# Spreading the depthwise convolution of the next image over five chunks and moving its group norm, tables, offsets and pixels later

## What is computed

```python
# block 0: group norm, 1x1 to 128 channels, a 3x3 depthwise convolution whose
# nine weights per channel come from the pooled image, mish, 1x1 back to 64
xh = conv1x1(gn(x), w_in, b_in)
hcx = relu(mean(xh) @ kg_w1.T + kg_b1)
kernels = (hcx @ kg_w2.T + kg_b2).reshape(b, c, 3, 3)
y = depthwise(xh, kernels)
x = x + conv1x1(y * tanh(softplus(y)), w_out, b_out)
# block 1: group norm again, then a deformable 3x3 convolution
v = gn(x)
offset, mask = conv3x3(v, w_off) + b_off, sigmoid(conv3x3(v, w_mask) + b_mask)
val = bilinear(v, own position + tap + offset) * mask      # nine taps
z = conv1x1(concat(sum_taps(w_def, val), offset, mask), w_1x1) + b_1x1
x = x + silu(batchnorm(z))
```

## Time and profile before

| | |
|---|---|
| median of 3 runs | 5547.52 us (5545.2 to 5550.46) |
| profiled execution | 5541.43 us |
| its span from first to last instruction | 5539.6 us |
| mean granted TensorE clock | 0.815 of full speed |
| busy: PE, DVE, ACT, POOL | 81%, 81%, 47%, 73% |

### The profile page before, as it was taken

How to read it: one execution, slowest core, us unless ns; L and a number is a source line. 1 busy time by engine, 2 the same in 40 slices (tenths; PEclk the granted TensorE clock), 3 DMA queues, 4 the chain that set the end, 5 groups by cost and what they waited for, 6 DMA issues and landing times.

```text
span 5539.6 us, 46074 instructions
## 1 busy us (share of the span) xinstructions
PE 4466.2 (81%) x14774; PEld 1996.3 (36%) x14774; DVE 4498.5 (81%) x5310; ACT 2595.6 (47%) x3580; POOL 4041.9 (73%) x4243
## 2 busy tenths in 40 slices
PE   8688787888878888788887878887778887888874
PEld 3233343433434333333333433333333343333331
...
GB/s 106 103 118 135 103 133 122 120 131 105 141 111 131 123 109 143 104 131 123 116 136 105 133 123 120 133 103 139 115 132 123 110 144 105 131 115 114 122 107 101
DMA packets 280991, 667.35 MB, mean 120 GB/s; under 512 B 76191, under 2 KB 118058, under 8 KB 278506
## 3 DMA queue, kind: packets, MB, share of 16 engines
...
## 4 chain that ended last, share of the span: by engine, by line
PE 36%; DVE 25%; POOL 22%; issue 12%; ACT 3%; DMA 2%; DVEq 0%; POOLq 0%; SPq 0%; ACTq 0%
POOL gat L504 22%; PE yo_ps L774 12%; PE tap_ps L774 7%; DVE gat L1371 5%; PE z_ps L696 5%; DVE pairs L1350 5%; DVE conv_ps L1241 4%; DVE hat_s L1398 4%; PE tap_ps L690 2%; DMA gat<-patch_table,ixu 2%; PE conv_ps L588 2%; PE conv_ps L568 2%; DVE uc L1248 1%; PE xh_ps L756 1%; DVE conv_ps L1238 1%
## 5 line engine op out<-in xcount | busy, mean ns | idle before, releaser
L504 POOL DMA_INDIRECT gat<-patch_table,ixu x4236 | 4033.6, 952 | 1483.6 <-issue 1261.8
L1371 DVE TENSOR_TENSOR gat<-gat,wgt_ps 128x1024 f32<-128x1024 f32 x1059 | 1283.9, 1215 | 445.9 <-DMA gat<-patch_table,ixu 438.7
L1350 DVE TENSOR_REDUCE pairs<-gat 128x256 f32<-128x1024 f32 x1024 | 1239.4, 1210 | 0.0
L774 PE MATMUL yo_ps<-hat_s,hat_image 128*128 128x512 f32 x1860 | 1007.0, 695 | 7.0 <-issue 7.0
L774 PE MATMUL tap_ps<-hat_s,hat_image 128*128 128x512 f32 x1860 | 895.1, 631 | 0.0
L690 PE MATMUL tap_ps<-ident,pairs 128*128 128x128 f32 x2048 | 393.3, 324 | 572.6 <-DVE pairs L1350 572.4
L1039 ACT ACTIVATE val<-tap_ps 128x512 f32<-128x512 f32 x512 | 303.3, 592 | 1087.9 <-PE tap_ps L690 1087.7
L774 PEld LDWEIGHTS yo_ps<-hat_s,hat_image 128*128 128x128 f32 x1860 | 417.5, 232 | 603.5 <-issue 594.2
L1241 DVE SCALAR_TENSOR_TENSOR conv_ps<-xh,kb,conv_ps 128x1024 f32<-128x1024 f32 x480 | 617.5, 1286 | 12.7
L690 PEld LDWEIGHTS tap_ps<-ident,pairs 128*128 128x128 f32 x2048 | 271.1, 163 | 886.1 <-DVE pairs L1350 716.9
L774 PEld LDWEIGHTS tap_ps<-hat_s,hat_image 128*128 128x128 f32 x1860 | 360.5, 202 | 427.6 <-issue 417.8
...
## 6 DMA issues: line engine op xcount, KB each, us to landing
gat<-patch_table,ixu POOLq DMA_INDIRECT x4236, 2.7
...
hat_image<-patch_table SPq DMA_DIRECT2D x144, 128.0 KB
out<-n_z SPq DMA_DIRECT2D x128, 128.0 KB, 2.4
...
```

The lines of the kernel that those rows point to most:

```text
L504: pool.indirect_dma_start(gat[:, k, t * 2 * REC:(t + 1) * 2 * REC], None, table_rows, bass.IndirectOffsetOnAxis(ixu[:, i, k, t:t + 1], 0)) ...
L774: m = pe.matmul(hat_sums[t % 2][:, :], hat_image[:, q // NCH % 2, i, t, :], hat_s[:, i, :], start=(i == 0), stop=(i == HI - 1))
L1350: dve.tensor_reduce(total, gat[:, k, :].rearrange("p (t x c h) -> p t c x h", t=TILES, x=2, h=2), mybir.AxisListType.XY, ALU.add).then_inc ...
L1371: dve.tensor_tensor(patch, patch, wk.rearrange("p (n h) -> p n h", h=2).unsqueeze(2).to_broadcast([128, TILES * 2, C, 2]), ALU.mult).then_ ...
```

## The change

The plans are replaced. The convolution's twelve rows, until now three in each of chunks 0 to 3, are spread over chunks 0 to 4 (3, 3, 2, 2, 2); products, residuals and mish steps follow them; the statistics of the residual become a step of their own (`statistics`), later than the residual; `group_mean` moves from after tap 3 of chunk 4 to its end, `group_var` and `normalise` from chunk 4 to the first two taps of chunk 5; the tables, offsets and pixels stand two to three taps later than before, and `points 0` and `points 1` one tap later. Chunk 7 is as it was.

```diff
+PLAN_CONV = (
+    ((1, "convolve 0 0"), (2, "convolve 0 1"), (4, "convolve 0 2"), (5, "exp 0"), (6, "ln 0"), (7, "tanh 0"), (8, "project 0")),
+    ((1, "residual 0"), (2, "convolve 1 0"), (4, "convolve 1 1"), (7, "convolve 1 2"), (8, "exp 1"), (8, "finish")),
+    ((1, "ln 1"), (2, "tanh 1"), (3, "project 1"), (5, "residual 1"), (5, "statistics 0"), (6, "convolve 2 0"), (8, "convolve 2 1"), (8, "finish")),
+    ((1, "convolve 2 2"), (2, "exp 2"), (3, "ln 2"), (4, "tanh 2"), (5, "project 2"), (6, "statistics 1"), (7, "residual 2"), (8, "convolve 3 0"),
+     (8, "finish")),
+    ((1, "convolve 3 1"), (2, "convolve 3 2"), (3, "exp 3"), (4, "ln 3"), (4, "statistics 2"), (5, "tanh 3"), (6, "project 3"), (8, "residual 3"),
+     (8, "statistics 3"), (8, "finish"), (KK, "group_mean")),
 )
...
-PLAN_NORM = ((1, "project"), (3, "residual"), (4, "group_mean"), (5, "group_var"), (6, "normalise"), (8, "finish"))
 PLAN_PREPARE = (
-    ((1, "last_row"), (1, "offsets 0"), (2, "to_table 0"), (2, "x_stats 0"), (3, "to_table 1"), (4, "offsets 1"), (4, "to_pixels 0"),
-     (5, "to_table 2"), (5, "x_stats 1"), (6, "to_table 3"), (7, "to_pixels 1"), (8, "to_table 4"), (8, "finish")),
-    ((1, "offsets 2"), (2, "to_table 5"), (2, "points 0"), (3, "offsets 3"), (3, "to_pixels 2"), (4, "points 1"), (4, "to_table 6"),
-     (5, "x_stats 2"), (5, "to_table 7"), (6, "points 2"), (6, "to_pixels 3"), (7, "x_stats 3"), (8, "finish")),
+    ((1, "group_var"), (2, "normalise"), (2, "x_stats 0"), (4, "last_row"), (4, "offsets 0"), (5, "to_table 0"), (5, "x_stats 1"), (6, "to_table 1"),
+     (7, "offsets 1"), (7, "to_table 2"), (8, "to_pixels 0"), (8, "finish"), (KK, "to_table 3")),
+    ((1, "to_table 4"), (1, "offsets 2"), (2, "to_pixels 1"), (3, "to_table 5"), (3, "points 0"), (4, "offsets 3"), (4, "to_table 6"), (5, "points 1"),
+     (5, "to_pixels 2"), (5, "to_table 7"), (5, "x_stats 2"), (6, "points 2"), (7, "to_pixels 3"), (7, "x_stats 3"), (8, "finish")),
...
             def to_pixels(n, s):
                 pe.wait_ge(om_done, n * NCH + s * 2 + 2)
+                pe.wait_ge(px_done, n * NCH + s * 2 + 1)
...
                 if s > 0 and row == 0:
-                    dve.wait_ge(mished, n * NCH + s * 2)
+                    dve.wait_ge(x1_done, n * NCH + s * 2 + 1)
...
+            def statistics(n, s):
+
+                for j in range(2):
+                    q = n * NCH + s * 2 + j
+                    dve.wait_ge(x1_done, q + 2)
+                    dve.bn_stats(stat1[:, bass.ds(s * 2 + j, 1), :].rearrange("p o s -> p (o s)"), xb[:, n % 2, span(s * 2 + j)]).then_inc(st_done, 1)
```

More of the change, by code:

```diff
@@ L115, in plan_of @@
 def plan_of(b, g):
-    if g == 0:
-        plan = PLAN_START[0] if b == 0 else PLAN_FIRST
-    elif g < 4:
-        plan = PLAN_START[g] if b == 0 and g < 3 else PLAN_BLOCK0
-    else:
-        plan = PLAN_NORM if g == 4 else PLAN_PREPARE[g - 5]
+    plan = PLAN_CONV[g] if g < 5 else PLAN_PREPARE[g - 5]
+    if b == 0 and g < len(PLAN_START):
+        plan = by_unit(plan, PLAN_START[g])
     q = b * NCH + g
@@ L138, in group @@
             done = units
-        name, _, number = step.partition(" ")
+        name, *numbers = step.split()
         if name in steps:
-            steps[name](b, g, int(number or 0))
+            steps[name](b, g, *(int(i) for i in numbers))
     if done < KK:
@@ L1118, in image @@
             def image(b, more, further):
-                steps = {"exp": lambda b, g, i: exp(b + 1, g), "ln": lambda b, g, i: ln(b + 1, g), "tanh": lambda b, g, i: tanh(b + 1, g),
-                         "group_var": lambda b, g, i: group_var(b + 1), "normalise": lambda b, g, i: normalise(b + 1),
-                         "last_row": lambda b, g, i: last_row(b + 1), "to_table": lambda b, g, i: to_table(b + 1, i),
-                         "next_indices": lambda b, g, i: next_indices(b + 1),
+                steps = {"exp": lambda b, g, i: exp(b + 1, i), "ln": lambda b, g, i: ln(b + 1, i), "tanh": lambda b, g, i: tanh(b + 1, i),
+                         "group_var": lambda b, g: group_var(b + 1), "normalise": lambda b, g: normalise(b + 1),
+                         "last_row": lambda b, g: last_row(b + 1), "to_table": lambda b, g, i: to_table(b + 1, i),
+                         "next_indices": lambda b, g: next_indices(b + 1),
                          "offsets": lambda b, g, i: offsets_two(b + 1, i), "to_pixels": lambda b, g, i: to_pixels(b + 1, i)} if more else {}
@@ L1475, in image @@
             def image(b, more, further):
-                steps = {"convolve": lambda b, g, i: convolve(b + 1, g, i),
-                         "project": lambda b, g, i: project(b + 1, g - 1),
-                         "residual": lambda b, g, i: residual(b + 1, g - 1), "group_mean": lambda b, g, i: group_mean(b + 1),
-                         "group_var": lambda b, g, i: group_var(b + 1), "normalise": lambda b, g, i: normalise(b + 1),
+                steps = {"convolve": lambda b, g, i, row: convolve(b + 1, i, row),
+                         "project": lambda b, g, i: project(b + 1, i),
+                         "residual": lambda b, g, i: residual(b + 1, i), "statistics": lambda b, g, i: statistics(b + 1, i), "group_mean": lambda b, g: group_mean(b + 1),
+                         "group_var": lambda b, g: group_var(b + 1), "normalise": lambda b, g: normalise(b + 1),
                          "points": lambda b, g, i: points(b + 1, i)} if more else {}
```

67 lines of the change are left out of this document (32 added, 35 removed).

## The result

| | before | after |
|---|---|---|
| median | 5546.36 us (5540.84 to 5550.46, 4 runs) | 5691.35 us (5689.74 to 5693.49, 4 runs) |
| profiled execution, its span | 5541.43, 5539.6 us | 5693.49, 5691.7 us |
| mean granted TensorE clock | 0.815 | 0.821 |

The ratio is 1.0264, with a 95% interval of 1.0252 to 1.0276: 2.6% slower. All runs compared here are fast ones; a single run of the kernel before, taken beside e5 to e8, lasted 9187.51 us and is left out of the ratios. The prediction was 5715 us in a range of 5590 to 5800.

The account below looks back on a forecast made before the run. POOL's DMA issue pace was taken as the bound. Images become one chain of 92.4 + 52 + 205.3 = 349.7 us, +12 us for 14 passages: 5541 + 168 = 5709, plus 6 for the median, 5715 us; range 5590 to 5800.

Parts of the forecast that it names:

- The bound: POOL's indirect DMAs at 1.250 us each set the pace; 84 us of transpose waits are removable, floor 5457 us.
- Part 1: Chunks 0 to 4: spreading the convolution alone gains about 1 us an image; 205.3 us to DVE's chunk 5 against 202.0.
- The wait for tanh ahead of `project 0`: Chunk 0: `project 0` waits for a tanh that ScalarE can only do after `val`, 1 us.
- Part 2: Chunks 5 and 6: late normalise delays pixels 1 to 62.5 us after DVE's chunk 5 copy; DVE waits some 20 us.
- lag: DVE's copy at a chunk's start less POOL's first issue of it; at chunk 7 forecast 24 us instead of 9.
- the 278.8 us of POOL's: POOL's waits on the transposes, forecast to rise from 112 to about 280 us, now also ahead of chunks 1 and 2.
- drain: Extra of about 1.38 us per ScalarE table switch, left out of the sum; with it about 5735 us in the end.
- 47 us as the point: Time after DVE's chunk 5 copy by which `points 0` needs its pixels for DVE to reach chunk 6's last gather in time.
- the balance wins: Rival: pixels in chunks 5 and 6 come early enough, only the spreading counts; 5530 us, or 5463; chance 0.10.
- The size: Each image costs 12 us more over 14 passages, +168 us on the profiled 5541, plus 6 for the median.
- PE cold: Rival: PE idles at DVE's waits and runs offsets and chunk 7 at the lower clock; 5790 us; chance 0.06.
- Half of it: Rival: normalise and offsets early enough that the chunk 7 lag grows only 4 to 8 us; 5590 us; chance 0.08.

Follow-up runs that it names:

- e5: Kernel before with only the tables, offsets and pixels of chunks 5 and 6 at the change's later taps, group norm early: 5597.39 us, ratio 1.0084.
- e8: Kernel before with only the third convolution row of chunks 1 to 3 two taps later, mish behind it: 5549.16 us, ratio 0.9996.
- e4: Kernel before with convolution rows of chunks 1 to 3 after taps 2, 4 and 6 instead of 2, 3 and 4, mish behind: 5456.67 us, ratio 0.9842.
- e9: Kernel before with convolution rows of chunks 1 to 3 after taps 2, 5 and 6, mish after tap 7: 5457.8 us, ratio 0.9847.
- e3: Changed kernel with the convolution back at its old places, late group norm and later taps kept: 5685.93 us, ratio 1.0254.
- e6: Kernel before with only the late group norm; tables, offsets, pixels at old taps, except chunk 5's first, directly behind normalise: 5684.92 us, ratio 1.0244.

## Why the prediction was right, point by point

- **The bound.** POOL's pace is the floor, and the waits above it are what an order can change. e4 and e9 reach the 5457 us that I named as the least; the profiled execution of e9 took 5454.0, so that figure holds to some 3 us and is no strict floor.
- **Part 1.** The sum for chunks 0 to 4 was 205.3 us; it is 204.2, with chunk 0 at 45.0 (46.4 said), 1 at 40.7 (40.4), 2 at 43.0 (42.8), 3 at 38.9 (38.5) and 4 at 36.6 (37.2). So the spreading pays for chunks 1 and 3 in chunk 0, and e3 confirms that it decides nothing. Inside the right sum for chunk 0 there is luck. The wait for tanh ahead of `project 0`, 1 us in the text, is 5.77 us in image 5 (L1249 at 1937.72) and 4.17 in image 6, 5.0 on average, and still the chunk is 1.4 us shorter than said. So the rest of that sum was 5.4 us too long. Some 2 to 4 us of it are VectorE's wait for the hat's product at the end of chunk 0 (2.09 us in image 6, 3.74 in image 5), which is in the 39.3 that I started from and is gone in after; the rest I can't assign. In chunk 2 the wait is 5.7 (5.5 said); chunks 3 and 4 have 1.7 and 2.4 that I hadn't counted. The waits for tanh are 223 us in all, 15 an image and not 6.5.
- **Part 2, the chain up to the pixels.** Counted from the copy of chunk 5 (2104.74): normalise ends at 12.9 (13.7 said), the offsets' first copies at 27.2 (27.0), the second at 41.5 (41.9), offsets 2 and the hat's product at 57.7 (57.3), the copy of pixels 1 at 62.65 (62.5). VectorE's wait is 19.6 us (some 20), and chunk 7 begins at 92.1 (92.4) with a lag of 22.5 (24). Of the 16 waits at L1315 for ACT L1004, 15 are of 16.6 to 20.3 us; these waits, the 278.8 us of POOL's (about 280 said) and the lost waits for gathers at the end of chunk 6 are as forecast, as are the 30 more table loads (3610 ScalarE instructions for 3580). The new load on the chain has its step 1.29 us behind its start, so here too no drain is seen, and the 1.4 us that the Trainium skill (ScalarE: Activation LUTs, What ACT_TABLE_LOAD costs) would add didn't come.
- **The step that was incomplete.** I took the pixels' place in the queues for the only gate, and 47 us as the point from which it decides. For the changed kernel that was nearly right: POOL's chunk 7 at 69.5, plus the old lag of 9.1, less 29.4 of work is 49.2, and the pixels at 62.65 are the later gate by 2.8 us. What I left out is the second gate, `hat_g`, done at 62.4. It had the least slack before: VectorE's `hat_part` started at 52.0 and could start at 55.5, and it waited for `hat_g` there already, 5.41 us, which I had read only as the start of the work behind it. The pixels had far more slack: they were copied at 33.8 and, with the old lag at chunk 5, could be as late as 53. The number was right because `hat_g` came 2.8 us short of mattering in after, and that is luck: the prediction didn't reckon it. Where they come apart the omission shows. In e6 the pixels are there at 48.8, before their point, and I expected at most 5570 us; `hat_g` is done at 65.4 and the run took 5685. The rival "the balance wins" had less room than I gave it. I also hadn't split the loss between the late group norm and the later taps: 135 and 47, and 142 for both.
- **The size.** An image takes 11.3 us more, not 12, and the span grows by 152 us, which is 13.5 such images and not 14: 168 - 152 = 16 us. I added 6 us for the median over the profiled run, and it lies 2 below. That is the whole of 5715 - 5691.
- **The other rivals.** "PE cold" didn't happen: the offsets' products take 392.1 us in all against 404.3, and the granted clock is 0.821 against 0.815. "Half of it" (5590 us) is the time of e5, 5597, though there the lag at chunk 7 grows by 2.8 us and not by 4 to 8.
